# Gates of the second stage on 32 partitions, mask products on 64 rows, and pieces queued behind the rows of maxima

## What is computed

```python
def _mlstm_head(q, k, v, ig, fg, eps=1e-06):   # stage 2, 4 heads of 32
    log_f = jax.nn.log_sigmoid(fg)
    cs = jnp.concatenate([jnp.zeros((1, 1), log_f.dtype), jnp.cumsum(log_f, axis=0)], axis=0)
    log_d = jnp.where(jnp.tri(s, dtype=bool), (cs - cs.T)[1:, 1:] + ig.T, neg)
    m = jnp.max(log_d, axis=-1, keepdims=True)
    d = jnp.exp(log_d - m)
    c = q @ (k.T / jnp.sqrt(dh)) * d
    n = jnp.maximum(jnp.sum(c, axis=-1, keepdims=True), jnp.exp(-m))
    return c / (n + eps) @ v
# stages 5, 8 and 11, 16 heads of 8; 5 and 11 causal, 8 with a mask that is given
scores = jnp.einsum('bhqd,bhkd->bhqk', q, k) + mask
out = jnp.einsum('bhqk,bhkd->bhqd', jax.nn.softmax(scores, axis=-1), v)
```

## Time and profile before

| | us |
|---|---|
| median of three runs | 2344.24 |
| lowest and highest run | 2338.33, 2347.04 |
| the profiled execution's own time | 2333.73 |
| its span, first to last instruction | 2331.9 |
| PE busy | 1706.5 |
| DVE busy | 1234.4 |
| ACT busy | 869.3 |
| POOL busy | 460.1 |

### The profile page before, as it was taken

One profiled execution on the slowest core, in us unless ns is written; L12 is line 12 of the kernel. 1 busy time (PEld: TensorE's weight loads), 2 busy tenths in 40 slices (PEclk: granted clock), 3 DMA queues, 4 the chain that ended last, 5 costly groups with the idle time before them and its releaser, 6 DMA issues. The chain is left out here.

```text
span 2331.9 us, 34732 instructions
## 1 busy us (share of the span) xinstructions
PE 1706.5 (73%) x11928; PEld 1171.9 (50%) x11952; DVE 1234.4 (53%) x4310; ACT 869.3 (37%) x1799; POOL 460.1 (20%) x605
## 2 busy tenths in 40 slices
PE   3227844757878786866547987996776776899988
PEld 1106714334545476666433544764343564677666
DVE  4754545324542778875336652333555777666422
ACT  1131223433552356656423554342344331133423
POOL 0000000012200243433024300001220211655311
PEclk8665567657998798987768998987798885899979
DMA  2000000012100454666023200001211000000000
GB/s 82 0 9 1 0 8 20 0 57 56 47 17 6 145 203 162 209 225 217 7 87 83 66 17 10 0 0 56 53 45 36 26 1 1 1 2 3 2 1 19
DMA packets 79739, 115.42 MB, mean 49 GB/s; under 512 B 8416, under 2 KB 60384, under 8 KB 78816
## 3 DMA queue, kind: packets, MB, share of 16 engines
q0 software_dynamic: 18432, 67.38, 8.3%
q1 hardware_dynamic: 58560, 44.87, 7.0%
q10 hardware_dynamic: 2592, 1.18, 0.2%
HBM read 88.82 MB, written 1.05 MB: 39 GB/s over the span
## 5 line engine op out<-in xcount | busy, mean ns | idle before, releaser
L2159 POOL DMA_INDIRECT f_rows<-tree_table,f_index x128 | 131.8, 1030 | 328.3 <-DVE f_index L2215 206.1
L2372 PE MATMUL f_ps_o<-f_rows,shared_sb 128*128 128x128 f32 x1024 | 135.4, 298 | 68.0 <-ACT f_rows L2444 68.0
L2372 PEld LDWEIGHTS f_ps_o<-f_rows,shared_sb 128*128 128x128 f32 x1024 | 131.2, 212 | 73.5 <-ACT f_rows L2444 69.9
L1307 ACT ACTIVATE x_probs<-x_ps_z 128x768 f32<-128x768 f32 (+1 forms) x128 | 117.4, 917 | 132.3 <-PE x_ps_z L1172 72.6
L2444 ACT ACTIVATE f_rows<-f_rows,f_low_act 128x128 f32<-128x128 f32 x512 | 152.9, 386 | 0.8
L2254 DVE CUSTOM_DVE_ANT_0 f_rows<-f_rows,f_xn 128x128 f32<-128x128 f32 x512 | 111.3, 286 | 59.1 <-DMA f_rows<-tree_table,f_index 59.1
L1015 DVE TENSOR_REDUCE x_minus_max<-x_ps_s 128x4 f32<-128x1024 f32 x64 | 78.1, 1224 | 69.8 <-PE x_ps_s L1172 69.6
L1163 PE MATMUL x_ps_z<-x_queries,x_keys 64*128 64x256 bf16 (+1 forms) x512 | 48.4, 269 | 47.5 <-DMA x_queries<-x_max_pieces 29.1
L1632 PE MATMUL f_ps_h<-f_xnT,weights 128*128 128x512 f32 x144 | 76.4, 658 | 2.7 <-ACT f_hT L1697 2.7
L1307 ACT ACTIVATE a_probs<-a_ps_z 128x768 f32<-128x768 f32 x64 | 51.9, 811 | 69.5 <-PE a_ps_z L1169 69.5
L1644 PEld LDWEIGHTS f_ps_y<-weights,f_hT 128*128 128x128 f32 x576 | 70.1, 192 | 14.3 <-issue 12.6
(11 more groups left out here) (624 smaller groups left out, 4317.8 us busy)
## 6 DMA issues: line engine op xcount, KB each, us to landing
x_queries<-x_pieces SPq DMA_DIRECT2D x96, 64.0 KB, 2.1
x_keys<-x_pieces SPq DMA_DIRECT2D x84, 64.0 KB, 2.1
a_queries<-a_pieces SPq DMA_DIRECT2D x48, 64.0 KB, 2.1
weights<-w_L_ffn SPq DMA_DIRECT2D x1, 2985.5 KB, 10.1
a_keys<-a_pieces SPq DMA_DIRECT2D x42, 64.0 KB, 2.0
weights<-w_L_ffn SPq DMA_DIRECT2D x1, 2449.0 KB, 10.6
weights<-w_L_ffn SPq DMA_DIRECT2D x1, 2176.0 KB, 10.5
f_rows<-tree_table,f_index POOLq DMA_INDIRECT x128, 6.0
```

The lines of the kernel that those rows point to most:

```text
L1307: a.activation(probs[:, r % HELD, :, :], ps_z[:, :, 0:WIDE], ACT.Exp, scale=scale).then_inc(exped, 1)
L2159: pool.indirect_dma_start(rows[:, u % 2, j, tree, :], None, g.tree_table, bass.IndirectOffsetOnAxis(index[:, u % 2, low, j * TREES + tree: ...
L2372: last = pe.matmul(ps_o[:, low, j, :], g.ident, rows[:, u % 2, j, tree, OUT + f * D:OUT + (f + 1) * D], start=k == 0, stop=k == TREES * FA ...
```

## The change

1. Stage 2: the gates lie on 32 partitions, row 4u + h for sequence u and head h, 256 columns each. The stationary operands `gates_x` and `gates_c` are built by VectorE with zeros around each unit's columns, and 16 products add up in one bank; `xn` and the transposes' bank are double (the second is a bank of `ps_kq`). ScalarE reads the gates once. The rows' operations are 32 x 256, one scan each; 4 products make the columns, 4 copies put them in place. GpSimd makes the stationary operands of the maxima's products (`minus_pick`, 32 x 4096) in one operation ahead of `v_ones`. The loops are written out.
2. Causal stages 5 and 11: identity and masks are stored by halves (`eyes`, `masks`), and each mask product becomes two on 64 rows, the pair's heads on different halves.
3. Stages 5, 8 and 11: SyncE stacks unit u+2 in slot 8u+8, behind the rows of maxima of unit u.

```diff
+    UNITS = B
+    ROWS = UNITS * NH
     I_AT = 32
+    APART = 2 * ROWS + NH
...
-        xn, xnT = sb("xn", [P, TILES, D]), sb("xnT", [P, ALL])
-        gate_ctx = sb("gate_ctx", [P, I_AT + NH])
-        f_gate, f_log, f_sum = (sb(n, [NH, ALL]) for n in ("f_gate", "f_log", "f_sum"))
-        g_rows, m_rows, least = (sb(n, [NH, ALL]) for n in ("g_rows", "m_rows", "least"))
+        xn, xnT = sb("xn", [P, 2, TILES, D]), sb("xnT", [P, ALL])
+        gates_x, gates_c = (sb(n, [P, UNITS * APART]) for n in ("gates_x", "gates_c"))
+        f_gate, f_log, f_sum = (sb(n, [ROWS, T]) for n in ("f_gate", "f_log", "f_sum"))
+        g_rows, m_rows, least = (sb(n, [ROWS, T]) for n in ("g_rows", "m_rows", "least"))
+        ones, zeros, minus_pick = sb("ones", [ROWS, T]), sb("zeros", [ROWS, T]), sb("minus_pick", [ROWS, ROWS, P])
...
-        ps_g = ps_kq[:, 0, :]
+        ps_g = ps_kq[:, 0, 0:T]
+        ps_turn = (ps_t[:, :], ps_kq[:, 1, :])
...
-        cols_ps = ps_t[:, 0:NT * 2 * NH].rearrange("p (j k h) -> p j k h", j=NT, k=2)
+        cols_ps = ps_t[:, 0:2 * HALVES * ROWS].rearrange("p (k j r) -> p k j r", k=2, j=HALVES)
...
-        STARTS, FLOOR = g.seq_starts[0:NH, 0:COLS], w["seq_floor"][0:NH, :]
-        turns = [slice(t * COLS, (t + 1) * COLS) for t in range(TURNS)]
...
+            pool.tensor_scalar(minus_pick[:, :, :], g.ident[0:ROWS, 0:ROWS].rearrange("p (r o) -> p r o", o=1).broadcast_to([ROWS, ROWS, P]),
+                               -1.0, None, ALU.mult).then_inc(picks_ready, 1)
...
-            v.tensor_tensor(gate_ctx[:, :], w["gates_k"], w["gates_v"], ALU.add).then_inc(weights_ready, 1)
-            with v.Fori(0, TURNS) as t:
-                v.wait_ge(xT_made, t)
-                normalise(v, g, t, xn).then_inc(xn_ready, 1)
+            by_unit = lambda a, at: a[:, :].rearrange("p (u k) -> p u k", k=APART)[:, :, at:at + NH]
+            for_units = lambda a, at: a[:, at:at + NH].rearrange("p (o h) -> p o h", o=1).broadcast_to([P, UNITS, NH])
+
+            def normalise_turn(t):
+                if t >= 2:
+                    v.wait_ge(xT_made, t - 1)
+                for j in range(TILES):
+                    n = t * TILES + j
+                    last = v.tensor_scalar(xn[:, t % 2, j, :], g.x[:, n, :], g.moments[:, n, 0:1], g.rstd[:, n:n + 1],
+                                           ALU.subtract, ALU.mult)
+                last.then_inc(xn_ready, 1)
+
+            normalise_turn(0)
+            v.memset(gates_x[:, :], 0.0)
+            v.memset(gates_c[:, :], 0.0).then_inc(cleared, 1)
+            v.wait_ge(cleared, 1)
+            for at in (0, I_AT):
+                v.tensor_copy(by_unit(gates_x, at), for_units(w["gates_x"], at))
+                last = v.tensor_tensor(by_unit(gates_c, at), for_units(w["gates_k"], at), for_units(w["gates_v"], at), ALU.add)
+            last.then_inc(weights_ready, 1)
+            for t in range(1, TURNS):
+                normalise_turn(t)
             gate_step = Chain(v, gate_steps)
+            v.memset(ones[:, :], 1.0)
+            gate_step(v.memset(zeros[:, :], 0.0))
             v.wait_ge(flog_ready, 1)
             gate_step(v.scalar_tensor_tensor(f_log[:, :], f_gate[:, :], 0.0, f_log[:, :], ALU.min, ALU.subtract))
-            for part in turns:
-                last = v.tensor_tensor_scan(f_sum[:, part], STARTS, f_log[:, part], 0.0, ALU.mult, ALU.add)
-            gate_step(last)
+            gate_step(v.tensor_tensor_scan(f_sum[:, :], ones[:, :], f_log[:, :], 0.0, ALU.mult, ALU.add))
             gate_step(v.tensor_tensor(g_rows[:, :], g_rows[:, :], f_sum[:, :], ALU.subtract))
-            for part in turns:
-                last = v.tensor_tensor_scan(m_rows[:, part], FLOOR, g_rows[:, part], -1e30, ALU.add, ALU.max)
-            gate_step(last)
+            gate_step(v.tensor_tensor_scan(m_rows[:, :], zeros[:, :], g_rows[:, :], -1e30, ALU.add, ALU.max))
             v.tensor_tensor(least[:, :], f_sum[:, :], m_rows[:, :], ALU.add).then_inc(sum_ready, 1)
             v.wait_ge(cols_made, 1)
-            gate_step(v.tensor_copy(all_cols[:, :, :, :], cols_ps))
+            for k in range(2):
+                for half in range(HALVES):
+                    last = v.tensor_copy(all_cols[:, half::HALVES, k, :], cols_ps[:, k, half, :].rearrange("p (u h) -> p u h", h=NH))
...
-            with pe.Fori(0, TURNS) as t:
-                now = bass.ds(t * COLS, COLS)
+
+            def turn_tokens(t):
                 pe.wait_ge(xn_ready, t + 1)
-                pe.wait_ge(xnT_ready, t)
+                if t >= 2:
+                    pe.wait_ge(xnT_ready, t - 1)
                 for j in range(TILES):
-                    last = pe.transpose(ps_t[:, j * P:(j + 1) * P], xn[:, j, :], g.ident)
+                    last = pe.transpose(ps_turn[t % 2][:, j * P:(j + 1) * P], xn[:, t % 2, j, :], g.ident)
                 last.then_inc(xT_made, 1)
+
+            def add_gates(t):
                 pe.wait_ge(xnT_ready, t + 1)
-                pe.wait_ge(gates_ready, t)
-                pe.matmul(ps_g[0:I_AT + NH, :], w["gates_x"], xnT[:, now], start=True, stop=False)
-                pe.matmul(ps_g[0:I_AT + NH, :], gate_ctx[:, :], g.ctxT[:, now], start=False, stop=True).then_inc(gates_made, 1)
+                for u in range(t * SEQS, (t + 1) * SEQS):
+                    for k, (weights, of) in enumerate(((gates_x, xnT), (gates_c, g.ctxT))):
+                        last = pe.matmul(ps_g[0:2 * ROWS, :], weights[:, u * 2 * ROWS:(u + 1) * 2 * ROWS], of[:, u * T:(u + 1) * T],
+                                         start=u == 0 and k == 0, stop=u == UNITS - 1 and k == 1)
+                last.then_inc(gates_made, 1)
+
+            turn_tokens(0)
+            for t in range(TURNS):
+                if t + 1 < TURNS:
+                    turn_tokens(t + 1)
+                add_gates(t)
             pe.wait_ge(least_ready, 1)
-            for j in range(NT):
-                for k, rows in enumerate((g_rows, least)):
-                    last = pe.matmul(cols_ps[:, j, k, :], rows[:, j * P:(j + 1) * P], g.ident[0:NH, 0:NH],
+            pe.wait_ge(xnT_ready, TURNS)
+            for k, rows in enumerate((g_rows, least)):
+                for half in range(HALVES):
+                    last = pe.matmul(cols_ps[:, k, half, :], rows[:, half * P:(half + 1) * P], g.ident[0:ROWS, 0:ROWS],
                                      start=True, stop=True)
             last.then_inc(cols_made, 1)
...
-                    last = pe.matmul(ps_m[:, h, :], w["minus_head"][0:NH, h * P:(h + 1) * P],
-                                     m_rows[:, bass.ds(t * COLS + s * T, T)], start=True, stop=True)
+                    last = pe.matmul(ps_m[:, h, :], minus_pick[:, (t * SEQS + s) * NH + h, :], m_rows[:, :], start=True, stop=True)
...
-            with a.Fori(0, TURNS) as t:
-                now = bass.ds(t * COLS, COLS)
+            for t in range(TURNS):
                 a.wait_ge(xT_made, t + 1)
-                a.activation(xnT[:, now], ps_t[:, :], ACT.Copy).then_inc(xnT_ready, 1)
-                a.wait_ge(gates_made, t + 1)
-                a.activation(f_gate[:, now], ps_g[0:NH, :], ACT.Identity, bias=w["fbias"])
-                a.activation(g_rows[:, now], ps_g[I_AT:I_AT + NH, :], ACT.Identity, bias=w["ibias"]).then_inc(gates_ready, 1)
+                a.activation(xnT[:, t * COLS:(t + 1) * COLS], ps_turn[t % 2], ACT.Copy).then_inc(xnT_ready, 1)
+            a.wait_ge(gates_made, TURNS)
+            a.activation(f_gate[:, :], ps_g[0:ROWS, :], ACT.Identity, bias=w["fbias"])
+            a.activation(g_rows[:, :], ps_g[I_AT:I_AT + ROWS, :], ACT.Identity, bias=w["ibias"]).then_inc(gates_ready, 1)
             step = Chain(a, act_steps)
...
+            eyes, masks = sb("eyes", [P, 2, P], BF16), sb("masks", [P, 2, 4, P], BF16)
         else:
+            ident16 = sb("ident16", [P, P], BF16)
...
-                if v_in(slot) is not None:
-                    stack(v_in(slot))
-                if v_in(slot) == 0:
+                if v_in(slot - 1) is not None:
+                    stack(v_in(slot - 1))
+                if v_in(slot - 1) == 0:
...
-            v.tensor_copy(ident16[:, :], g.ident)
             if causal:
+                by_half = lambda m: w[m].rearrange("p (i k) -> p i k", i=2)
+                v.tensor_copy(eyes[:, :, :], by_half("eyes"))
                 for i, m in enumerate(causal):
-                    last = v.tensor_copy(masks[:, i, :], w[m])
+                    last = v.tensor_copy(masks[:, :, i, :], by_half(m))
                 last.then_inc(const_ready, 1)
             else:
-                v.nop().then_inc(const_ready, 1)
+                v.tensor_copy(ident16[:, :], g.ident).then_inc(const_ready, 1)
...
-                for i in range(2):
-                    if causal:
-                        last = pe.matmul(by_parts(banks[:, i, 0:WIDE]), ident16[:, :], masks[:, 2 * kind:2 * kind + 2, :],
-                                         start=False, stop=True)
```

(17 more changed lines are left out.)

27 lines of the change are left out of this document (13 added, 14 removed).

## The result

The changed kernel takes 2255.01 us (median of four runs, 2251.63 to 2263.8), the kernel before 2341.53 in runs on the same chip: a ratio of 0.9634, 95% interval 0.9599 to 0.9669. The forecast was 2252, in the range 2234 to 2273. The total hides that two of its terms were wrong, as the stages show. (What is called stage 11 here and ahead of the result, `layer3_latent_attention`, is the tenth of the twelve in order of time; the name is kept.)

The account below looks back on a forecast made before the run. Bounds seen: stage 2's single-operation chain and TensorE at clock 0.50, and queue order in stages 5 and 11. Terms -31.8 - 3.5 - 18.1 - 36.5 - 2 = -91.9 gave 2241.8, with 10.5 to the median 2252; range 2234 to 2273.

Parts of the forecast that it names:

- Stage 2's rows: Stage 2, last read of the gates to first spreading of maxima: 9.7 us against 41.5, -31.8.
- Stage 2's turns: Stage 2, the four turns up to the gates' last read: end at 155 instead of 158.90, given as -3.5.
- VectorE's turn 0 takes 4 x 0.29: Stage 2's start: four normalisations at two per 0.58 us, so TensorE begins at about 140.2.
- 14.6 us bound of GpSimd's time: Stage 2, `minus_pick`: 3.8 us at the copy's rate or 14.6 at a tensor_scalar's, hidden in either case.
- The rival of the lock: Stage 2: GpSimd's `minus_pick` blocks VectorE's turn 0 for up to 14.6 us, total 2266; chance 0.16.
- The maxima ahead of the pieces: Stages 5, 8, 11: rows of maxima issued first; -18.1 for first sequences, -36.5 for steady units of 5 and 11.
- the queue now sets a pace: Stages 5 and 11: SyncE's issues and landing set 16.0 us a unit; stage 5 bound by TensorE's 16.5.
- The masks: Causal stages 5 and 11: mask products on halves run at once, hides start some 0.09 us earlier; net -2.
- The untouched stages: All stages other than 2, 5, 8 and 11: no difference, 0.
- The rival of a slower kernel: Stages 5 and 11: units take 27 us through SyncE's closed chain, total 2360; chance 0.02.
- ring: Attention units: SyncE's closed chain of rows, pieces, landing, GpSimd's split, `score`, maxima; over 0.5% slower needs 26.6 us a unit.
- rivals on the clock: Stage 2's loop: the clock rises as 32 rows work where 4 did, -24, total 2228; chance 0.05.

Follow-up runs that it names:

- late_pick: The changed kernel with GpSimd starting `minus_pick` only when all four turns are normalised; 2247.88 us, ratio 0.9592 to the kernel before.

## Why the prediction was right, and where it was not

- **Stage 2's rows**, -31.8: measured 41.5 to 9.9, -31.6. Most terms were read off a record of the same width. The scans took 0.68 for 256 columns where half of 1.14 gave 0.57, the products 1.73 for 1.7.
- **Stage 2's turns**, -3.5: measured +5.1 (163.97 - 137.34 against 21.5), wrong by 8.6. The step that failed is "VectorE's turn 0 takes 4 x 0.29": `minus_pick` held it for 10.6 us. A second part was too dear: the forecast added 3.6 us to the 11.2 of TensorE for a slow clock in the first turns (151.4 to 155), and the loop took 11.5 (granted clock 0.83) and, in late_pick, 12.4 (0.76). And 137.4 to 155 is 17.6, so the term by its own working is -3.9 and not -3.5. With GpSimd behind the normalisations (late_pick) the turns take 152.09 - 136.70 = 15.4 us against 21.5, so without the hold this term would have been -6. The 14.6 us bound of GpSimd's time was an outer one; it took 10.57.
- **The rival of the lock**, 0.16, is what happened, at +11 (5.1 in place of -6.1) and not +14. The case against it rested on one coincidence of two records; the earlier trace rows had the same kind of VectorE operation held to the end of a float32 copy. Of the two, the row with float32 on both sides and a hold in it was the nearer. The Trainium skill's rule ("SBUF — State Buffer", "Who interferes with whom"), that whichever of the two issues first gets the shared ports for the whole instruction and the other fully blocks, gave the right side here. As a lock for the whole instruction it holds for `minus_pick`, memset, copy and `tensor_tensor`; two-operation `tensor_scalar` let two thirds of the normalisations through, and there the measurement decides. The order doesn't agree either: the normalisation that was held began 0.08 us ahead of `minus_pick`.
- **The maxima ahead of the pieces**, -54.6: 54.8 alone by the times, 53.4 by the stages. The first sequence's wait is 1.4 to 1.5 us in stages 5 and 11, as worked out (1.3), and 0.2 in stage 8. Stage 5's units were forecast at 16.5 and took 16.3, stage 11's 16.0 and 15.8. The mechanism is right as a chain; "the queue now sets a pace" is not to be read as a full queue, for SyncE waits 5.6 us a unit.
- **The masks**, net -2: 0 alone, and with the new order no gain that is clear of the scatter. The mechanism (products of halves at once, masks 0.10 us sooner behind `score`) is in the rows above; that the 0.10 is a change of tiling less is the forecast's reading and wasn't tried apart.
- **The untouched stages**, 0: +8.8 in the profiled execution. 3.3 of it is stage 4 at a lower granted clock, in every kernel with part 1, and a term that the forecast lacks; the scatter covers the rest.
- The total: the four stages lost 5.4 of the 91.9 that were forecast. The lock's +11 stood against turns that were worth 2.6 more without it and against stages 5 and 8, which gave 2.4 and 1.1 more (stage 11 gave 1.0 less); the turns' wide margin in the forecast (155 where 151.4 was worked out) covered part of the lock by chance. The number 2252 owes a part of its nearness to that. The rival of a slower kernel stays out: its ring is the bound, but at 16.3 a unit and not 25.
- Of the rivals on the clock: stage 2's loop stayed at 0.50 and 82.10 us.

## What to carry to other kernels

Where one DMA queue serves both a result that is waited for and loads for later, write the urgent one first, and then count the issues behind it up to what waits for the last of them: here thirteen, some 9 us, in a chain of 16 that closes once a unit. Each more is paid in full, though the queue stands idle for a third of the time; how full a queue is doesn't tell whether its issues cost. Work that is moved to an "idle" GpSimd isn't hidden until one has looked at what VectorE does at that moment: place it where VectorE waits anyway (one line, 10 us), or on ScalarE. And a saving inside a period that a wait closes is worth next to nothing while the wait is there.
